# A two-layer block on one core: first stage in parts, first attention unit begun among the last expert tiles, feed-forward steps of the last stage at other places

## The chip, the cores and the metric

The kernel runs on one core of a Trainium2 chip. A core has five engines, each with its own queue of instructions, worked off strictly in order: TensorE (PE in the rows; its weight loads are PEld), VectorE (DVE), ScalarE (ACT), GpSimd (POOL) and SyncE (SP, which here only issues transfers). They wait for each other through semaphores. Data lies in an on-chip buffer of 128 partitions, and TensorE writes into eight accumulator banks. The metric is the time of one execution on the device in microseconds. Three runs of the kernel before took 1812.76, 1813.0 and 1818.22 us, with a median of 1813.0 us.

## The reference

The input is x, 8 sequences of 256 tokens of width 256: 2048 tokens. The program computes two transformer layers, and each adds two branches to its input, both fed by the same layer norm:

```python
xn = layernorm(x)
x = x + L0_attn(xn) + L0_ffn(xn)
xn = layernorm(x)
x = x + L1_attn(xn) + L1_ffn(xn)
```

- `L0_attn` is a delta rule over 16 heads of 128: projections q, k, v, a causal convolution of 4 taps and a SiLU on each, then a recurrence over the tokens, `state += k (beta (v - k state))`, output `q state`, a norm and a projection.
- `L0_ffn` has a shared MLP for every token, and 8 routed experts of which each token uses 2. The router takes a sigmoid of `xn @ router`, chooses two of four groups, then two experts, and weights their outputs.
- `L1_attn` learns at test time: per pair of heads and chunk of 64 tokens it forms gradients of three 128x128 weights, passes each through two Newton-Schulz steps (`A = X X'; B = b A + c A A; X = a X + B X`), adds them to the weights, rescales these, and answers the queries with the new weights.
- `L1_ffn` chooses 2 of 6 experts for each of the 8 sequences: up-projection, GELU, down-projection, weighted sum.

## The kernel before

The order of the work is written out by hand, engine by engine. Each step is a small function of the same name on several engines (TensorE multiplies, ScalarE or VectorE fetches the result from a bank and gives the bank back). The program has these stages, one after the other:

1. **Norm, router, shared MLP** (0 to 109 us). SyncE loads x in four parts of 512 tokens (g = 0 to 3), all counted on one semaphore `s_x`, then 11 small constants, then weights. VectorE waits for all four parts, takes the statistics of all (`norm_stats`, L1866 to L1873), and then normalizes part by part (`norm_rows`, L1882, into `xnr`). GpSimd takes the inverse roots between them (L2583). TensorE turns each part (`ln_turn`, L574, 8 instructions' worth of matmul time per part), and ScalarE and VectorE each fetch one half of it into `xnT` (L1383, L1888). When all parts are turned, TensorE computes the router and beta logits (L621, 64 narrow matmuls). ScalarE takes the sigmoid, and VectorE does the routing, a chain of 38 small dependent instructions (L1924 to L1966), the result of which (`slots`, L1960) lets GpSimd send 2 x 16 blocks of token rows to their slots in device memory (L2594). SyncE then reads the rows back, tile by tile (L500). Meanwhile TensorE works on the shared MLP: `shared_up` (L632, L638), whose result ScalarE passes through SiLU (L1391) and VectorE multiplies (L1977), and `shared_down` (L650). The matmul of the fourth piece (L638) needs the bank that the first of these products gives back, and all the products stand behind the whole routing on VectorE.
2. **Expert tiles** (109 to 207 us). 39 tiles of 128 rows run in a pipeline of four steps on TensorE: `turn_x` (L682), `expert_up` (L690), `turn_h` (L699), `expert_down` (L709). The tile j uses bank j % 2 for its turn.
3. **Layer 0 attention** (207 to some 1360 us). 64 units of 512 tokens and one head, in `period`s in which five units overlap. A unit begins with `project` of queries (QRY), keys (KEY) and values (VAL) on TensorE (L737), the first tap on ScalarE (`tap0`, L1433), three more on VectorE (`tap`, L2020), and the SiLU on ScalarE (L1437). Queries and values share bank 0.
4. **Layer 1 attention and its feed-forward.** 16 units x0 to x15 (a pair of heads and sequences in a chunk), of which four run interleaved. Each unit's Newton steps for s = 0 (two weights at once) and s = 1 (the third) are `TURN` (L1017), `GRAM`, `SQUARE` and `NEXT` (all L1012) on TensorE, with a copy on ScalarE after `TURN` and `GRAM` (L1612, L1615) and an operation on VectorE after `SQUARE` and `NEXT` (L2265, L2268). After them come `turn_weight`, `gate_queries`, `turn_mixed`, `output` and `turn_output`. In the last stretch, from 1719 us, the feed-forward of the eight sequences is laid between the steps of x13 to x15: `up(b)` (L1111) on TensorE, `gelu(b)` on ScalarE (L1661), `weigh(b)` on VectorE (L2188), `down(b)` (L1129, with the output projection of the attention in L1131), and `add_results(b)` (L2194) on VectorE. SyncE begins to load the weights of the chosen experts when unit x12 is out, two experts for each sequence, in four buffers (L541 to L548). A load for sequence b + 4 begins when `down(b)` is done.

ScalarE holds the functions of one table set at a time, and GELU and SiLU lie in different ones: the program has an `ACT_TABLE_LOAD` wherever it goes from one to the other.

## Time and profile before

| | us |
|---|---|
| median of three runs | 1813.0 |
| the profiled execution's own time | 1812.96 |
| its span, first to last instruction | 1811.2 |
| TensorE busy | 1700.7 (94% of the span) |
| VectorE busy | 1493.7 (82%) |
| ScalarE busy | 1199.3 (66%) |
| GpSimd busy | 1102.8 (61%) |

The profile shows one execution. A busy share is an average over stages that have different limits; which wait counts is read from the chain of waits and from the order of time in that stage. The profile also has the clock that was granted to TensorE, as a share of full speed, in any stretch (1.00 is 2.4 GHz, 0.50 is 1.2 GHz).

### The profile page before, as it was taken

The page shows a single profiled execution, that of the slowest core. Times are in us where ns is not written, and L with a number is a line of the kernel's source. Part 1 is how long each engine was busy: PE and PEld are TensorE (multiplying, and loading weights), DVE is VectorE, ACT ScalarE, POOL GpSimd, SP SyncE. Part 2 cuts the span into 40 slices and gives each one's busy share as a digit, 9 for nine tenths or more (in the row PEclk, how much of TensorE's full clock was granted, in tenths as well). Part 3 has the DMA queues.
Part 4 walks back from the last instruction along what each step waited for, and adds up shares of the span by engine and source line. Part 5 has one row for each costly group of instructions (what it writes and reads, how often), then busy time and mean ns, then how long its engine had stood idle before and what let it go on. Part 6 is the DMA issues. An engine that isn't in the chain of part 4 may idle for free.

```text
span 1811.2 us, 41460 instructions
## 1 busy us (share of the span) xinstructions
PE 1700.7 (94%) x14070; PEld 1236.6 (68%) x14070; DVE 1493.7 (82%) x3496; ACT 1199.3 (66%) x2907; POOL 1102.8 (61%) x1148
## 2 busy tenths in 40 slices
PE   5999899999999999999999999999987788888878
PEld 4477557777777777777777777777766566666666
DVE  5322499999999999999999999999986788888843
ACT  1124467777777777777777777777754588778853
POOL 1510057777777777776666666666665578777731
PEclk8999999999999999999999999999988799999999
DMA  9323400110110101100000000011002000000032
GB/s 309 137 83 108 121 22 27 32 38 24 32 35 21 38 20 35 29 24 29 23 18 23 26 15 29 15 26 29 15 1 59 1 1 1 2 1 1 1 89 88
DMA packets 66097, 73.83 MB, mean 41 GB/s; under 512 B 10976, under 2 KB 54768, under 8 KB 65776
## 3 DMA queue, kind: packets, MB, share of 16 engines
q1 hardware_dynamic: 62919, 63.92, 12.2%
q0 software_dynamic: 3072, 8.65, 1.5%
q8 instruction: 49, 0.80, 0.2%
q14 instruction: 57, 0.46, 0.1%
HBM read 55.45 MB, written 17.10 MB: 40 GB/s over the span
## 4 chain that ended last, share of the span: by engine, by line
PE 82%; DVE 8%; ACT 5%; issue 2%; POOL 1%; SPq 1%; DMA 0%; ACTq 0%; POOLq 0%; DVEq 0%
PE banks L737 19%; PE banks L880 6%; PE banks L749 4%; PE banks L836 3%; PE banks L757 3%; PE banks L855 3%; PE banks L765 3%; PE banks L794 3%; PE banks L808 3%; PE banks L690 3%; PE banks L802 2%; PE banks L936 2%; PE banks L801 2%; PE banks L709 2%; PE banks L1012 2%
## 5 line engine op out<-in xcount | busy, mean ns | idle before, releaser
L737 PE MATMUL banks<-xnT,hw 128*128 128x512 f32 x768 | 414.0, 622 | 4.0 <-DVE cv L2020 4.0
L2061 DVE CAST_PREDICATED MM<-lmask,banks 128x512 bf16<-128x512 uint32 x384 | 272.1, 709 | 34.4 <-PE banks L802 30.3
L2020 DVE SCALAR_TENSOR_TENSOR cv<-banks,hc,cv 128x510 f32<-128x510 f32 (+2 forms) x384 | 284.3, 741 | 10.8 <-ACT cv L1433 6.1
L1483 ACT ACTIVATE T<-banks 128x256 bf16<-128x256 f32 x384 | 149.7, 390 | 145.2 <-PE banks L794 144.2
L2665 POOL TENSOR_TENSOR X<-X,yrow 128x512 f32<-128x512 f32 x128 | 163.2, 1275 | 66.5 <-ACT yrow L1515 66.5
L2629 POOL TENSOR_TENSOR kn<-nsum,half_pos 128x4 f32<-128x4 f32 x64 | 65.5, 1023 | 148.5 <-DVE nsum L2032 148.5
L802 PEld LDWEIGHTS banks<-MM,T 128*128 128x128 bf16 x1536 | 104.1, 98 | 65.2 <-issue 48.0
L801 PEld LDWEIGHTS banks<-T,MM 128*128 128x128 bf16 x1280 | 99.0, 97 | 65.4 <-ACT T L1483 63.2
L880 PE MATMUL banks<-ho,OT 128*128 128x256 f32 x512 | 143.1, 403 | 0.0
L794 PEld LDWEIGHTS banks<-MM,Gb 128*128 128x128 bf16 x1536 | 79.2, 98 | 93.7 <-DVE MM L2061 54.0
L2020 DVE SCALAR_TENSOR_TENSOR cv<-banks,hcv,cv 128x510 f32<-128x510 f32 (+2 forms) x192 | 141.2, 736 | 0.8 <-ACT cv L1433 0.7
L1515 ACT ACTIVATE yrow<-banks,oinv 128x256 f32<-128x256 f32 x256 | 107.0, 472 | 50.7 <-POOL oinv L2660 47.8
L802 PE MATMUL banks<-MM,T 128*128 128x64 bf16 x1536 | 136.3, 193 | 0.5 <-ACT T L1483 0.5
L1437 ACT ACTIVATE raw<-cv 128x512 f32<-128x512 f32 x192 | 121.9, 635 | 4.1 <-DVE cv L2020 3.5
L737 PEld LDWEIGHTS banks<-xnT,hw 128*128 128x128 f32 x768 | 116.8, 191 | 8.7 <-issue 6.7
L801 PE MATMUL banks<-T,MM 128*128 128x64 bf16 x1280 | 118.4, 193 | 2.5 <-ACT T L1483 2.5
L794 PE MATMUL banks<-MM,Gb 128*128 128x64 bf16 x1536 | 109.8, 194 | 3.3 <-DVE MM L2061 3.3
L2066 DVE TENSOR_TENSOR Rb<-Rm,banks 128x256 bf16<-128x256 f32 x256 | 106.2, 415 | 5.0 <-POOL Rm L2656 4.1
L2660 POOL TENSOR_TENSOR oinv<-orr,half_neg 128x4 f32<-128x4 f32 x64 | 66.0, 1032 | 52.8 <-ACT orr L1493 52.8
L808 PE MATMUL banks<-Rb,MM 128*128 128x128 bf16 x640 | 89.0, 221 | 6.2 <-DVE Rb L2066 3.8
L880 PEld LDWEIGHTS banks<-ho,OT 128*128 128x128 f32 x512 | 88.3, 192 | 6.9
L1433 ACT ACTIVATE cv<-banks,hc 128x512 f32<-128x512 f32 x128 | 89.2, 697 | 2.4 <-PE banks L737 2.4
(318 smaller groups left out, 4880.7 us busy)
## 6 DMA issues: line engine op xcount, KB each, us to landing
MM<-in_eye SPq DMA_DIRECT2D x64, 256.0 KB, 2.7
slot_rows<-zeros SPq DMA_DIRECT2D x1, 5304.0 KB, 20.4
xs<-slot_rows SPq DMA_DIRECT2D x13, 408.0 KB, 3.9
slot_out<-ye SPq DMA_DIRECT2D x13, 384.0 KB, 2.7
hw<-in_hw SPq DMA_DIRECT2D x16, 256.0 KB, 3.5
wT<-in_winit SPq DMA_DIRECT2D x8, 384.0 KB, 4.5
wgu<-in_wgu SPq DMA_DIRECT2D x1, 2816.0 KB
w1c<-in_ew SPq DMA_DIRECT2D x16, 176.0 KB
```

Of the source, the lines that this page charges most:

```text
L737: ins = pe.matmul(PROJ[t][:], hw[:, kk, t, :], xnT[:, kk, u.b * BLK:(u.b + 1) * BLK], start=(kk == 0), stop=(kk == KD - 1))
L794: last = pe.matmul(o[:, k * 64:(k + 1) * 64], Gb[:, par, k, :], strips(MM[:, u.b, 0, k, :], size, 0, 1), start=True, stop=True)
L801: pe.matmul(o[:, k * 64:(k + 1) * 64], MM[:, u.b, 1, k, :], strips(T1[:, k, :], size, 0, 1), start=True, stop=True)
L802: last = pe.matmul(o[:, (TILES + k) * 64:(TILES + k + 1) * 64], T1[:, k, :], strips(MM[:, u.b, 1, k, :], size, 1, 1), start=True, stop=True)
L808: last = pe.matmul(solve_bank(u)[:, s * P:(s + 1) * P], MM[:, u.b, 1, s * NC + c, :], rhs[:, s, :], start=True, stop=True)
L880: last = pe.matmul(bank[7 - s][:, c * D:(c + 1) * D], OT[:, s * NC + c, :], ho[:], start=True, stop=True)
L1437: act.activation(raw[:, u.b % 2, t, :], cv[:, t, :], ACT.Silu).then_inc(act_silu, 1)
L1483: act.activation(strips(T1[:].rearrange("p i t -> p (i t)"), LEVELS[lv], 0, 1), grams_bank(u)[:, 0:TILES * 64].rearrange("p (k e) -> p k e ...
L1515: last = act.activation(yrow[:, s, c], bank[7 - s][:, c * D:(c + 1) * D], ACT.Copy, scale=oinv[:, u.b % 2, s * NC + c:s * NC + c + 1])
L2020: dve.scalar_tensor_tensor(o, y, taps_of(t)[:, TAPS - 1 - i:TAPS - i], o, ALU.mult, ALU.add).then_inc(dve_conv, 1)
L2061: dve.copy_predicated(dst, m, ps).then_inc(dve_mm, 1)
L2665: pool.tensor_tensor(xs, xs, yrow[:, s], ALU.add).then_inc(pool_x, 1)
```

## The change

**First stage by parts.** Each of the first two parts of x has a semaphore of its own, and the last two share a third. VectorE takes the statistics of part 1 and then normalizes part 0, and so on, instead of all statistics first. ScalarE fetches both halves of every turned part. TensorE computes the logits of part g - 1 behind the turn of part g. VectorE's first two products of the shared MLP stand within the routing instead of behind it.

**First unit.** TensorE projects queries and keys of unit 0 in the tile pipeline's rounds 38 and 39, with the first taps on ScalarE, and the other taps on VectorE around the last `keep_h`. Tiles turn into bank 1 - j % 2, so that the bank of each projection is free. The periods leave these steps out for unit 0.

**Last stage.** The steps `up`, `gelu`, `weigh`, `down` and `add_results` stand at other places between the steps of x13 to x15 on the three engines: `up(0)` and `up(1)` later, and the others around them. Near the end `turn_output(x15)` stands ahead of `up(7)`, and `square_outputs(x15)` and `keep_turned(x15)` ahead of `gelu(6)` and `gelu(7)`.

```diff
@@ loads
-...[:, g * TPB:(g + 1) * TPB, :]).then_inc(s_x, 16)
+...[:, g * TPB:(g + 1) * TPB, :]).then_inc((s_x, s_x1, s_x2, s_x2)[g], 16)
@@ TensorE, first stage
-            for g in range(NBLK):
+            ln_turn(0)
+            for g in range(1, NBLK):
                 ln_turn(g)
+                logits(g - 1)
+            logits(NBLK - 1)
@@ TensorE, tile pipeline
                     expert_up(n - 1, experts[n - 1])
+                if n in (TILES0 - 1, TILES0):
+                    for kk in range(KD):
+                        project(first_unit, QRY if n < TILES0 else KEY, kk)
                 if 0 <= n - 2 < TILES0:
                     turn_h(n - 2)
@@ ScalarE, first stage and tile pipeline
                 act.activation(turned_place(0, 0, g), turned_from(0, 0, g), ACT.Copy).then_inc(ln_kept0, 1)
+                act.activation(turned_place(0, 1, g), turned_from(0, 1, g), ACT.Copy).then_inc(ln_kept1, 1)
...
+                if n in (TILES0 - 1, TILES0):
+                    tap0(first_unit, QRY if n < TILES0 else KEY)
                 if 0 <= n - 3:
                     weigh_y(n - 3)
+                if n == TILES0 + 1:
+                    silu(first_unit, QRY)
+            silu(first_unit, KEY)
@@ VectorE, first stage
+            dve.wait_ge(s_x, 16)
+            norm_stats(0, 0)
+            dve.wait_ge(s_x1, 16)
+            norm_stats(1, 0)
+            norm_rows(0, 0)
+            dve.wait_ge(s_x2, 32)
+            norm_stats(2, 0)
+            norm_rows(1, 0)
+            norm_stats(3, 0)
+            norm_rows(2, 0)
+            norm_rows(3, 0)
...
             step(dve.tensor_scalar(r_w[:], r_w[:], SCALE0, None, ALU.mult))
+            shared_product(0)
...
+            shared_product(1)
             dve.wait_ge(*s_places)
@@ VectorE, tile pipeline
+                if n == TILES0:
+                    tap(first_unit, QRY, 1)
+                    tap(first_unit, QRY, 2)
+            tap(first_unit, QRY, 3)
+            for i in range(1, TAPS):
+                tap(first_unit, KEY, i)
@@ ScalarE, last stage
             newton(x15, 0, 1, TURN)
+            gelu(0)
             newton(x15, 0, 1, GRAM)
             keep_weight(x14, 0)
             keep_turned(x13)
             square_weights(x14, 1)
+            gelu(1)
             keep_weight(x14, 1)
@@ VectorE, last stage
             newton(x14, 1, 1, SQUARE)
+            weigh(0)
             newton(x14, 1, 1, NEXT)
```

How the instructions stand in the built programs, at the places where they move. On TensorE, in the first stage of the kernel before (L574 turns a part, L621 is the logits, L632 and L638 begin the shared MLP):

```order
L574 MATMUL banks<-ident,xnr 128x128 x32
L621 MATMUL banks<-wbr,xnT 128x24 x32
L632 MATMUL banks<-xnT,wsg 128x512 x2
L638 MATMUL banks<-xnT,wsu 128x512 x2
```

and of the changed kernel, where the same steps are L579, L624, L642 and L648:

```order
L579 MATMUL banks<-ident,xnr 128x128 x16
L624 MATMUL banks<-wbr,xnT 128x24 x8
L579 MATMUL banks<-ident,xnr 128x128 x8
L624 MATMUL banks<-wbr,xnT 128x24 x8
L579 MATMUL banks<-ident,xnr 128x128 x8
L624 MATMUL banks<-wbr,xnT 128x24 x16
L642 MATMUL banks<-xnT,wsg 128x512 x2
L648 MATMUL banks<-xnT,wsu 128x512 x2
```

The logits moved up between the turns, and only those of parts 2 and 3 still stand behind the last turn.

On TensorE, at the end of the tile pipeline of the changed kernel (L735 is `project`, L709 `turn_h`, L719 `expert_down`, L700 `expert_up`):

```order
L735 MATMUL banks0<-xnT,hw 128x512 x2
L709 MATMUL banks2<-ident,he 88x128 x2
L719 ISA
L719 MATMUL banks3<-wde,heT 128x256
L719 ISA
L719 MATMUL banks3<-wde,heT 128x256
L700 ISA
L700 MATMUL banks1<-wgu,xT 128x352
L700 ISA
L700 MATMUL banks1<-wgu,xT 128x352
L735 MATMUL banks0<-xnT,hw 128x512 x2
```

In the kernel before, all projections of unit 0 stand behind the last tile (L737 there). Two of the three moved ahead of the last three `turn_h` and `expert_down` steps.

On TensorE, in the last stretch of the kernel before (`XX2`, `banks2` are those of x14, `XX3`, `banks3` those of x15, L936 `gate_queries(x13)`, L1111 `up`):

```order
L936 MATMUL banks1<-w021,qkT1 64x256 x4
L1111 MATMUL banks0<-xnT,w1c 128x256 x4
L1111 MATMUL banks0<-xnT,w1c 96x256 x2
L1017 MATMUL banks2<-identb,XX2 128x128 x4
L1111 MATMUL banks0<-xnT,w1c 128x256 x4
L1111 MATMUL banks0<-xnT,w1c 96x256 x2
L1012 MATMUL banks2<-XX2 128x128 x4
L1017 MATMUL banks3<-identb,XX3 128x128 x8
```

and of the changed kernel, 13 rows further on in the same sequence (L1025 is `GRAM`, `SQUARE` or `NEXT`, L1030 `TURN`, L1093 `turn_output(x13)`, L1072 `turn_weight(x14, 0)`, L1124 `up`):

```order
L1025 MATMUL banks3<-Bm3,XX3 128x128 x8
L1124 MATMUL banks0<-xnT,w1c 128x256 x4
L1124 MATMUL banks0<-xnT,w1c 96x256 x2
L1025 MATMUL banks2<-ln_row 128x128 x4
L1030 MATMUL banks3<-identb,XX3 128x128 x8
L1093 MATMUL banks1<-ident,sg11 128x128 x2
L1025 MATMUL banks2<-Bm2,XX2 128x128 x4
L1025 MATMUL banks3<-XX3 128x128 x8
L1072 MATMUL banks2<-ident,wT2 128x128 x4
L1025 MATMUL banks3<-ln_row 128x128 x8
L1124 MATMUL banks0<-xnT,w1c 128x256 x4
L1124 MATMUL banks0<-xnT,w1c 96x256 x2
```

`up(0)` and `up(1)` moved from right behind `gate_queries(x13)` to behind the first Newton step of x15 and behind its second `SQUARE`.

## Rows read from the trace of the kernel before

**Rows 1.** The page: busy time of TensorE and VectorE.
```profile
PE 1700.7 (94%) x14070; PEld 1236.6 (68%) x14070; DVE 1493.7 (82%) x3496; ACT 1199.3 (66%) x2907; POOL 1102.8 (61%) x1148
```

**Rows 2.** Order of time, first stage: start, duration, engine, instruction, idle before.
```profile
9.64 1.40 DVE L1866 BATCH_NORM_STATS2 ln_st<-X 128x6 f32<-128x256 f32 x4 [9.64 <-DMA X<-in_x]
11.57 1.40 DVE L1866 BATCH_NORM_STATS2 ln_st<-X 128x6 f32<-128x256 f32 x4
21.41 1.37 DVE L1882 TENSOR_SCALAR xnr<-X,ln_mv,ln_rs 128x256 f32<-128x256 f32 x4
26.70 10.12 PE L621 MATMUL banks<-wbr,xnT 128*128 128x24 f32 x64 [0.88 <-DVE xnT L1888]
37.38 0.29 DVE L1924 TENSOR_TENSOR r_sfc<-sig,bias 128x128 f32<-128x128 f32 x1 [10.83 <-ACT sig L1385]
53.55 0.18 DVE L1960 CAST slots<-slotf 128x32 int32<-128x32 f32 x1
55.88 3.78 PE L638 MATMUL banks<-xnT,wsu 128*128 128x512 f32 x4 [3.40 <-DVE hT L1977]
98.36 1.45 SPq L500 DMA_DIRECT2D xs<-slot_rows  x3
108.70 0.60 PE L682 MATMUL banks<-ident,xs 128*128 128x128 f32 x4
```

**Rows 3.** The page's transfers: reading a group of tiles back, us to landing.
```profile
xs<-slot_rows SPq DMA_DIRECT2D x13, 408.0 KB, 3.9
```

**Rows 4.** TensorE in order of time, last stretch.
```profile
1727.87 2.86 PE L1111 MATMUL banks<-xnT,w1c 128*128 128x256 f32 x12 [1.93 <-DMA w2c<-in_eb]
1734.05 4.51 PE L1111 MATMUL banks<-xnT,w1c 128*128 128x256 f32 x12 [3.10 <-DMA w2c<-in_eb]
1745.14 0.62 PE L1012 MATMUL banks<-Bm,XX 128*128 128x128 bf16 x8
1751.03 0.66 PE L1059 MATMUL banks<-ident,wT 128*128 128x128 f32 x4
1800.70 2.84 PE L1129 MATMUL banks<-w2c,hs 128*128 128x256 f32 x12 [0.80 <-DVE hs L2188]
```

**Rows 5.** Transfers of x's four parts, then of wsg: issue to landing, us.
```profile
DMA to landing us min/median/max: 4.3/5.8/7.3
...
DMA to landing us min/median/max: 3.8/3.8/3.8
```

**Rows 6.** Stretches: length, TensorE busy, weight loads busy, granted clock, DMA share, GB/s.
```profile
18.80:20.80 2.00, 1.97 (x10) 1.94 (x11) 1.00 1.12 353
...
27.00:30.00 3.00, 3.00 (x29) 3.00 (x28) 1.00 1.20 429
31.00:34.00 3.00, 3.00 (x16) 3.00 (x15) 0.50 1.05 451
```

**Rows 7.** Weight loads of turns: in the first stage, then among the tiles.
```profile
L574 PEld LDWEIGHTS banks<-ident,xnr x32: 138/226/231, 18.8 to 25.4; 128*128 128x128 f32 x32
...
L682 PEld LDWEIGHTS banks<-ident,xs x66: 139/142/145, 110.6 to 189.9; 128*128 128x128 f32 x66
```

**Rows 8.** The chain of waits: start, duration, what; the first `shared_down`.
```profile
67.49 5.19 PE banks L650 x24
```

**Rows 9.** Order of time around the end of the tiles.
```profile
206.76 3.60 PE L737 MATMUL banks<-xnT,hw 128*128 128x512 f32 x8
210.42 4.53 DVE L2020 SCALAR_TENSOR_TENSOR cv<-banks,hc,cv 128x510 f32<-128x510 f32 x6 [4.93 <-ACT cv L1433]
218.02 3.70 PE L737 MATMUL banks<-xnT,hw 128*128 128x512 f32 x8
```

**Rows 10.** ScalarE and VectorE in order of time, last stretch.
```profile
1729.94 1.28 ACT L1661 ACT_TABLE_LOAD   x1 [3.56 <-PE banks L1111]
1731.24 1.19 ACT L1661 ACTIVATE hg<-banks,w2c 128x256 f32<-128x256 f32 x3
...
1807.91 0.69 DVE L2194 TENSOR_TENSOR X<-X,banks 128x512 f32<-128x512 f32 x1 [2.77 <-PE banks L1131]
```

More of the change, by code:

```diff
@@ L286, in do, with unbegun @@
                 step(u, *which)
+        first_unit = Unit(0, 0, 0)
+        def unbegun(u):
+            return None if u is not None and isinstance(u.n, int) and u.n == 0 else u
         def need(engine, signal, count):
@@ L612, in _, with logits @@
             pe.wait_ge(s_const, 11 * 16)
-            for g in range(NBLK):
-                ln_turn(g)
-            pe.wait_ge(ln_kept0, NBLK + 2)
-            pe.wait_ge(ln_kept1, NBLK + 2)
-            w = NH + E0
-            for t in range(NT):
-                for kk in range(KD):
-                    last = pe.matmul(bank[7][:, t * w:(t + 1) * w], xnT[:, kk, t * P:(t + 1) * P], wbr[:, kk, :],
-                                     start=(kk == 0), stop=(kk == KD - 1))
-            last.then_inc(pe_once, 1)
+            def logits(g):
+                pe.wait_ge(ln_kept0, g + 3)
+                pe.wait_ge(ln_kept1, g + 3)
+                w = NH + E0
+                for t in range(g * TPB, (g + 1) * TPB):
+                    for kk in range(KD):
+                        last = pe.matmul(bank[7][:, t * w:(t + 1) * w], xnT[:, kk, t * P:(t + 1) * P], wbr[:, kk, :],
+                                         start=(kk == 0), stop=(kk == KD - 1))
+                if g == NBLK - 1:
+                    last.then_inc(pe_once, 1)
+            ln_turn(0)
+            for g in range(1, NBLK):
+                ln_turn(g)
+                logits(g - 1)
+            logits(NBLK - 1)
             def shared_up(b):
@@ L710, in expert_down @@
                 last.then_inc(e_dn, 1)
-            experts = {}
-            for n in range(TILES0 + 3):
-                if n < TILES0:
-                    turn_x(n)
-                    experts[n] = pe.value_load(tile_e[0:1, n:n + 1], min_val=0, max_val=E0 - 1)
-                if 0 <= n - 1 < TILES0:
-                    expert_up(n - 1, experts[n - 1])
-                if 0 <= n - 2 < TILES0:
-                    turn_h(n - 2)
-                if 0 <= n - 3:
-                    expert_down(n - 3, experts.pop(n - 3))
             def project(u, t, kk):
@@ L739, in project @@
                     ins.then_inc(pe_proj, 1)
+            experts = {}
+            for n in range(TILES0 + 3):
+                if n < TILES0:
+                    turn_x(n)
+                    experts[n] = pe.value_load(tile_e[0:1, n:n + 1], min_val=0, max_val=E0 - 1)
+                if 0 <= n - 1 < TILES0:
+                    expert_up(n - 1, experts[n - 1])
+                if n in (TILES0 - 1, TILES0):
+                    for kk in range(KD):
+                        project(first_unit, QRY if n < TILES0 else KEY, kk)
+                if 0 <= n - 2 < TILES0:
+                    turn_h(n - 2)
+                if 0 <= n - 3:
+                    expert_down(n - 3, experts.pop(n - 3))
             def tokens(u, t, s, c):
@@ L1306, in _ @@
             turn_weight(x13, 1)
+            newton(x14, 0, 1, NEXT)
             spread_weights()
-            newton(x14, 0, 1, NEXT)
             gate_queries(x13)
-            up(0)
             newton(x14, 1, 0, TURN)
-            up(1)
             newton(x14, 1, 0, GRAM)
@@ L1324, in _ @@
             newton(x15, 0, 0, NEXT)
+            up(0)
             newton(x14, 1, 1, SQUARE)
@@ L1331, in _ @@
             newton(x15, 0, 1, SQUARE)
+            up(1)
             turn_weight(x14, 1)
+            newton(x15, 0, 1, NEXT)
             down(0)
-            newton(x15, 0, 1, NEXT)
             gate_queries(x14)
+            newton(x15, 1, 0, TURN)
             up(2)
-            newton(x15, 1, 0, TURN)
+            newton(x15, 1, 0, GRAM)
             down(1)
-            newton(x15, 1, 0, GRAM)
-            up(3)
             newton(x15, 1, 0, SQUARE)
@@ L1363, in _ @@
             down(5)
+            turn_output(x15)
             up(7)
-            turn_output(x15)
             down(6)
@@ L2003, in keep_h @@
                 dve.tensor_copy(heT[:, j % 2].rearrange("p i t -> p (i t)"), bank[4 + j % 2][0:FH0, 0:2 * P]).then_inc(e_hk, 1)
-            for n in range(TILES0 + 2):
-                if 0 <= n - 1 < TILES0:
-                    expert_h(n - 1)
-                if 0 <= n - 2:
-                    keep_h(n - 2)
             def tap(u, t, i):
@@ L2020, in tap @@
                 dve.scalar_tensor_tensor(o, y, taps_of(t)[:, TAPS - 1 - i:TAPS - i], o, ALU.mult, ALU.add).then_inc(dve_conv, 1)
+            for n in range(TILES0 + 2):
+                if 0 <= n - 1 < TILES0:
+                    expert_h(n - 1)
+                if 0 <= n - 2:
+                    keep_h(n - 2)
+                if n == TILES0:
[4 more added lines that the diff above has]
+                tap(first_unit, KEY, i)
             def key_sums(u, c):
```

115 lines of the change are left out of this document (52 added, 63 removed).

## The prediction, made before the changed kernel ran

> **What bounds the kernel now.** I read the page first: TensorE is busy for 94% of the span [rows 1], so what the change can win lies where TensorE waits or runs at half clock, at the start and at the end. I then read the order of time of the first 110 us, the stretches with their clock, the end of the tiles, and the last stretch engine by engine. In the first stage VectorE starts only when all of x is there, at 9.64. Everything up to the logits' end at 36.82 (26.70 + 10.12) hangs on that, the routing begins at 37.38, and the slots are ready at 53.73 [rows 2]. From there two chains run to the first tile. The sends let the read-back start at 98.36, which lands 3.9 later at 102.3 [rows 2, 3]. TensorE comes at 108.70 [rows 2]. The sends have a slack of 6.4 us. In the last stretch TensorE stands still for 1.93 and 3.10 us before `up(0)` and `up(1)`, until the experts' weights have landed, and all Newton steps are queued behind them [rows 4].
>
> The profiled execution took 1812.96 us, with 1.76 us outside its span, and the median is 1813.0: the sum can be made against either.
>
> **First stage.** The parts of x take 4.3 to 7.3 us from issue to landing [rows 5]. With the first issued at 0.75 us, it lands near 5.1 and the last at 9.64, so about 1.5 us apart. Statistics take 1.93 us a part (11.57 - 9.64) and normalizing takes 1.37 [rows 2]. From 5.1: statistics 0 to 7.0 and 1 to 8.9, rows 0 to 10.3, statistics 2 to 12.2, rows 1 to 13.6, statistics 3 to 15.5, rows 2 to 16.9, rows 3 to 18.3. The first turn also needs the last of the constants. These were issued just before wsg, which went out at 8.23 and landed 3.8 later [rows 5]. I put the constants at 11.0, an estimate.
>
> The first turn of 8 took 2.0 us [rows 6]; eight in a row at that pace (10 in 1.97) take some 1.8 with the last one's end. Logits are 16 matmuls a part: 29 ran in 3.00 us at full clock, so 1.65 us a part, and 16 in 3.00 us at half clock, so 3.0 a part [rows 6]. Over all 64 it was 10.12 us, or 2.5 a part [rows 2]. All slow: turn 0 to 13, turn 1 to 15.5, then logits, turn, logits, turn, logits, logits without a gap, 4 x 3.0 + 2 x 1.8 = 15.6, ends at 31.1. All fast, the last turn can begin at 18.3 and is followed by 1.2 + 2 x 1.65: 22.8. Which one? The granted clock reads 1.00 from 18.8 to 20.8, but a turn's weight load takes 226 ns there and 142 ns among the tiles, and the thin logits themselves were followed by 0.50 [rows 6, 7]. The durations decide for me: TensorE is slow in the first turns. But the logits took 2.5 a part, partly fast. By that figure for them the end is 15.5 + 4 x 2.5 + 2 x 1.8 = 29.1, and with the last two turns as short as the clock allows (1.4 less, by 142 ns against 226) 27.7. I take 28.3, 8.5 us earlier than 36.82.
>
> A rule bears on that row. The Trainium skill, TensorE: Matmul & The Clock Gate, part 1, says that the throttled state is the default and that activity releases it, and it warns that the trace's clock events are not always to be trusted. By that rule the turns start slow, as I took them. By the granted clock alone the logits would end at 22.8 and the sum would be 5.5 us less.
>
> Next, what the two products add. The chain from the first routing instruction to the slots took 53.73 - 37.38 = 16.35 us [rows 2]. The products are about as wide as the taps (0.76 us each [rows 9]), and a small part of them fills VectorE's wait for the counts of TensorE: 1.0 us more, bounds 0.8 and 1.5. That makes 17.35. The slots then come at 28.3 + 0.56 + 17.35 = 46.2, 7.5 us earlier. TensorE gains more: the wait of 3.40 before the fourth piece and the half clock behind it go. From the beginning of that wait, 55.88 - 3.40 = 52.48, to the first `shared_down` at 67.49 there are 20 matmuls in 15.0 us [rows 2, 8], and at 0.45 us each (3.60 for eight [rows 9]) they take 9.0. So TensorE arrives 8.5 + 6.0 = 14.5 us earlier, at 94.2. The sends arrive 7.5 earlier, at 94.8. They are now the later ones, and the first tile starts 108.7 - 94.8 = 13.9 us earlier. Bounds: 13.9 - 2.8 if the logits end at 31.1, 13.9 + 5.5 if at 22.8. No more than that is lost below unless the sends themselves get slower, since the moved instructions add no transfer. SyncE's queue holds the same transfers in the same order.
>
> **First unit.** Queries and keys are 8 of the matmuls of 0.45 us that stood behind the tiles (3.60 us) [rows 9]. They now stand between them. TensorE is full there, so the tiles end 3.6 us later, at 210.3 by the clock of the kernel before. What is gained is that the first tap, the three taps and the SiLU of the queries run beside the last tiles. VectorE does the taps at 0.76 us each (4.53 for six) [rows 9]. Two of them are in front of the last `keep_h`, which holds `expert_down(38)` by about 0.5 us. The query taps end at 210.4, the key taps at 212.8, the key SiLU at 213.4, the values' first tap at 214.1 (it stands behind that SiLU on ScalarE), and their three taps at 216.4. Unit 1's projection waits for that and began at 218.02 [rows 9]. That gives 1.6 us. Bounds: 2.7 if only the key chain counted, and -0.5 if the held `expert_down` and the late store of the last tiles cost as much as the chain wins. I take 1.6, from the row that the next unit waits on.
>
> **Last stage.** Removed from the path behind `gate_queries(x13)`: 1.93 + 2.86 + 3.10 + 4.51 = 12.4 us [rows 4]. Not all of that time is free. VectorE's scaling of x15 and the squares of x14's weights on ScalarE were finished in its shadow, and are late next: about 1.4 us. So `NEXT(x15, 0, 0)`, which ended at 1745.76, ends 11 us earlier, at 1734.8. Then `up(0)` and `up(1)` come back at full clock, 2.7 us each (the second ran at 4.51, slowed). `gelu(0)` stands on ScalarE ahead of x15's second `GRAM` copy, and needs 1.28 us for its table and 1.19 for itself [rows 10]: 2.2 us of new wait on TensorE. Other waits of some 1.9 us are covered by `up(0)`. At `turn_weight(x14, 1)`, which ended at 1751.69 [rows 4], I get -11.0 + 5.4 - 1.9 + 2.2 = -5.3 us. Behind it the remaining waits, the 0.80 before `down(6)` [rows 4] and some 2 us of small ones, are covered by feed-forward steps, and new ones cost about 0.5: -7.7. The weights of every sequence land before its `up`, since each `down(b)` that frees a buffer comes earlier too. I count some thirty hand-offs between engines at nothing in this walk, so I take -6.8. The last addition on VectorE, at 1807.91 [rows 10], then starts at 1801.1. Bounds: -11 if all small waits go, +1 if each of `gelu(0)` to `gelu(2)` holds the Newton steps behind it for its full 2.5 us and the later covers fail (-6.8 + 3 x 2.5 = +0.7).
>
> A rule speaks against this part. The Trainium skill, ScalarE: Activation LUTs, What ACT_TABLE_LOAD costs, gives a drain of 1.38 us besides the load of 1.28. In this trace the GELU starts 0.02 us behind the load [rows 10], so I count no drain. By the rule two exposed loads would make the sum 2.8 us more, 1793.5.
>
> **Sum.** 13.9 + 1.6 + 6.8 = 22.3, and 1813.0 - 22.3 = 1790.7 us.
>
> **Rivals.**
> 1. *TensorE is fast in the first stage.* The granted clock of 1.00 speaks for it [rows 6], the weight loads of 226 ns against it [rows 7]. The logits end at 22.8: 1790.7 - 5.5 = 1785.2 us.
> 2. *The last stage gives its gain back.* `weigh(b)` stands on VectorE ahead of Newton steps and waits for a GELU that waits for a table. TensorE's two waits of 5.0 us and the slow 1.7 us become waits of the Newton steps behind ScalarE. The load of 1.28 and the GELU of 1.19 [rows 10] speak for it, that these steps are queued once for each GELU. Against it, TensorE has an `up` or `down` of 2.7 to 3.5 us to do at most of them. Only 1 us is left of 6.8, and 1796.5 us comes out.
> 3. *The sends get slower.* They now begin at 47 us, while SyncE's bulk loads still run (DMA shares of 1.1 early on [rows 6]). If a quarter of the 32 sends take 0.5 us longer, the first tile starts 4 us later: 1794.7.
> 4. *Slower than before.* The 60 or so steady periods between 220 and 1360 us are bound by TensorE and by VectorE closely behind (94% and 82% [rows 1]). Unit 0 now enters with its queries and keys done, and the code before the loop has another length. If the units settle into another phase, or the loop's instructions are fetched later, each period pays. From 22.3 / 60 = 0.37 us per period on the kernel is slower; at 0.5 us it takes 1790.7 + 30 = 1820.7 us. Against it: the loop's text is the same, all its waits are between units, and a late start leaves no mark after one unit.
> 5. *The parts don't help*: if the constants, not x, held the first turn until 18 us, the first stage would win only the overlap of the logits and the products: some 6 us less, 1797. The landing of wsg at 12.0 [rows 5], behind them, speaks against it.
>
> **How the numbers follow.** The forecast, 1790.7, has 0.50; rival 1 0.13, rival 2 0.17, rival 3 0.10, rival 4 0.04, rival 5 0.04; no effect, by losses that cancel, 0.02. The forecast's own range, from the constants and the hand-offs, is 1787 to 1795. For 8 in 10 I take 1783 to 1800, which leaves out the lowest end of rival 1, the worst of rivals 2 and 3 together, and rival 4. A measurement of this kernel tells 0.3%, 5.4 us, from no change: faster 0.94, within it 0.02, slower 0.04.
>
> **What would show it.** In the changed profile: statistics from 5.1 us; the first turn at 11; the last logits at 28 with turn loads of 226 ns; the slots at 46; no wait before the fourth L648 matmul; the first tile (L692) at 95 with TensorE idle for 0.6 us before it; unit 1's projection 15.5 us earlier than 218.0; `up(0)` without a wait; ScalarE's `GRAM` copy behind the GELU's table load; the last addition on VectorE at 1785.6. It is wrong if the turns start after 13 us, if the tiles start before 92 or after 98, if the periods' length differs by more than 0.05 us, or if the last stretch shortens by less than 3 us.

## The result, and the profile after

| | median of its runs | ratio to before, 95% interval | profiled execution |
|---|---|---|---|
| before | 1813.85 us (6 runs, 1812.72 to 1818.22) | | 1812.96, span 1811.2 |
| changed | 1792.86 us (6 runs, 1791.16 to 1802.52) | 0.9891 [0.9876, 0.9906] | 1802.52, span 1800.7 |

The forecast was 1790.7 us (1783 to 1800). The change brings 21.0 us between the medians, or 1.09%.

The profiled execution is the slowest of the six, 9.7 us over their median. Lines of its page:

```profile
span 1800.7 us, 41462 instructions
PE 1710.1 (95%) x14070; PEld 1245.5 (69%) x14070; DVE 1490.8 (83%) x3492; ACT 1202.2 (67%) x2911; POOL 1104.9 (61%) x1148
PEclk9999999999999999999999999999987699999999
```

TensorE's busy time rose by 9.4 us against [rows 1], although it does the same 14070 matmuls. Where the same work takes longer, look at the clock. TensorE in order of time, first stage (start, duration, engine, line, what, idle before and who ended it):

```profile
11.48 3.72 PE L579 MATMUL banks<-ident,xnr 128*128 128x128 f32 x16 [11.48 <-DMA moec<-in_moec]
15.00 3.45 PE L624 MATMUL banks<-wbr,xnT 128*128 128x24 f32 x16
25.02 6.86 PE L624 MATMUL banks<-wbr,xnT 128*128 128x24 f32 x32
...
97.75 0.41 PE L692 MATMUL banks<-ident,xs 128*128 128x128 f32 x2 [0.93 <-DMA xs<-slot_rows]
98.63 0.43 PE L692 MATMUL banks<-ident,xs 128*128 128x128 f32 x2 [0.47 <-issue]
99.42 2.62 PE L700 MATMUL banks<-wgu,xT 128*128 x4 [0.35 <-issue]
```

The order is as forecast: first turn at 11.5, logits between the turns, rows from the sends as the last wait. But 16 logits took 3.45 us, 0.215 a piece, and the logits ended at 31.88, not at 28.3. Before they took 0.158 a piece [rows 2]. The first tile begins at 97.75 instead of 108.70, 10.95 us earlier. Behind the wait of 0.93 the first tiles are slow (2.62 us for the four that took 1.45 before); the granted clock is 0.61 from 99.4 to 103.8, and 1.00 behind it.

The second place is after the loop, two stretches in each of the two kernels (length, TensorE busy, clock, share of the transfers, GB/s); first before, then changed:

```profile
1420.00:1430.00 10.00, 7.57 (x44) 0.50 0.00 0
1430.00:1440.00 10.00, 6.43 (x71) 0.99 0.00 0
```
```profile
1420.00:1430.00 10.00, 7.22 (x53) 0.67 0.00 0
1430.00:1440.00 10.00, 9.22 (x64) 0.62 0.01 2
```

The changed kernel was 9.98 us ahead of the kernel before at its 1424 and 4.98 us ahead at its 1438, at the same instructions. Four matmuls of 512 columns that took 1.94 us before take 3.60 here (L960). Nothing in the change touches this place.

The last stretch, TensorE, then ScalarE:

```profile
1717.13 0.36 PE L1021 MATMUL banks<-gsum,onesP 128*128 128x12 f32 x2 [0.41 <-DVE gsum L2266]
...
1729.93 2.81 PE L1124 MATMUL banks<-xnT,w1c 128*128 128x256 f32 x12
...
1737.94 1.03 PE L1025 MATMUL banks<-ln_row 128*128 128x128 bf16 x8 [2.35 <-ACT ln_row L1635]
1738.77 4.08 PE L1124 MATMUL banks<-xnT,w1c 128*128 128x256 f32 x12
...
1796.40 1.03 PE L1144 MATMUL banks<-wpj,oT 128*128 128x256 f32 x4
```
```profile
1733.45 1.02 ACT L1632 ACTIVATE XX<-banks 128x1024 bf16<-128x1024 bf16 x1 [3.35 <-PE banks L1030]
1734.49 1.28 ACT L1681 ACT_TABLE_LOAD   x1
1735.78 1.19 ACT L1681 ACTIVATE hg<-banks,w2c 128x256 f32<-128x256 f32 x3
1736.87 1.02 ACT L1635 ACTIVATE ln_row<-banks 128x1024 bf16<-128x1024 f32 x1
```

The waits of 1.93 and 3.10 us of [rows 4] are gone. The forecast new wait behind `gelu(0)` is there, 2.35 us, and `up(1)` behind it takes 4.08 us instead of 2.81, at a granted clock of 0.64. From `total(x15)` (1717.13) to the end of `down(7)` it is 80.30 us. Before, these were at 1722.10 and 1807.87, 85.77 us.

One place marks the loop in both kernels: GpSimd's norm of the keys, once a unit (count, shortest/median/longest ns, start of the first and last); before, then changed:

```profile
L2629 POOL TENSOR_TENSOR kn<-nsum,half_pos x64: 1006/1027/1049, 219.2 to 1331.6; 128x4 f32<-128x4 f32 x64
```
```profile
L2656 POOL TENSOR_TENSOR kn<-nsum,half_pos x64: 1007/1029/1051, 208.6 to 1322.5; 128x4 f32<-128x4 f32 x64
```

### The profile page after: what moved, and what is told of

It is laid out like the page before. It is cut to its first block, busy times and chain, and to the rows that moved or that the text cites. A ratio compares the mean times of both kernels' runs of the same rounds, so it can differ in the third digit from the quotient of the medians.

```text
span 1800.7 us, 41462 instructions
## 1 busy us (share of the span) xinstructions
PE 1710.1 (95%) x14070; PEld 1245.5 (69%) x14070; DVE 1490.8 (83%) x3492; ACT 1202.2 (67%) x2911; POOL 1104.9 (61%) x1148
## 4 chain that ended last, share of the span: by engine, by line
PE 80%; DVE 9%; ACT 5%; POOL 3%; issue 2%; DMA 1%; SPq 0%; POOLq 0%; DVEq 0%; ACTq 0%
PE banks L735 19%; PE banks L893 6%; PE banks L762 4%; PE banks L770 3%; PE banks L849 3%; PE banks L868 3%; PE banks L778 3%; PE banks L807 3%; PE banks L821 3%; PE banks L700 3%; PE banks L815 2%; PE banks L949 2%; PE banks L814 2%; PE banks L1025 2%; PE banks L719 2%
## 5 line engine op out<-in xcount | busy, mean ns | idle before, releaser
L735 PE MATMUL banks<-xnT,hw 128*128 128x512 f32 x768 | 414.1, 622 | 2.5 <-DVE cv L2034 2.5
L735 PEld LDWEIGHTS banks<-xnT,hw 128*128 128x128 f32 x768 | 116.9, 191 | 6.5 <-DVE cv L2034 3.1
```

The source lines that it names most:

```text
L735: ins = pe.matmul(PROJ[t][:], hw[:, kk, t, :], xnT[:, kk, u.b * BLK:(u.b + 1) * BLK], start=(kk == 0), stop=(kk == KD - 1))
```

## The experiments

Twelve kernels ran, in four sets on four chips (B to E; the first two profiles are of A). Each set timed the kernel before as well: medians 1824.1 (B), 1822.2 (C), 1814.3 (D), 1823.7 (E). Because chips differ by 10 us, ratios are compared, and the profiles are cut at marks: end of the routing logits, start of the last send, first tile's turn, first and last norm of the keys, `total(x15)`, end of `down(7)`. The first three columns are times from the start, the other four are lengths from one mark to the next, in us.

| kernel | chip | ratio [95%] | logits end | last send | first tile | to 1st norm | loop | to total | last stretch |
|---|---|---|---|---|---|---|---|---|---|
| before | A | | 36.8 | 95.8 | 108.7 | 110.5 | 1112.4 | 390.5 | 85.8 |
| before_again | C | (one run, 1817.39) | 38.3 | 97.2 | 112.9 | 110.5 | 1112.5 | 390.7 | 85.8 |
| changed | A | 0.9891 | 31.9 | 91.8 | 97.8 | 110.9 | 1113.9 | 394.6 | 80.3 |
| after_again | C | 0.9882 [0.9858, 0.9906] | 24.0 | 83.9 | 100.9 | 108.6 | 1113.9 | 394.5 | 80.3 |
| e1_first_stage | B | 0.9933 [0.991, 0.9956] | 23.9 | 83.8 | 98.1 | 111.8 | 1114.0 | 389.2 | 85.7 |
| e2_first_unit | B | 0.9985 [0.9968, 1.0002] | 36.7 | 95.7 | 118.7 | 108.7 | 1113.7 | 391.9 | 89.3 |
| e3_last_stage | B | 0.9964 [0.9946, 0.9981] | 39.1 | 98.6 | 119.3 | 110.5 | 1112.4 | 394.5 | 80.3 |
| e4_warm | B | 0.9888 [0.9863, 0.9912] | 27.6 | 87.5 | 103.4 | 108.6 | 1113.9 | 394.6 | 80.3 |
| e5_gelu_later | C | 0.9891 [0.9868, 0.9914] | 31.7 | 91.6 | 104.7 | 108.7 | 1112.7 | 394.0 | 79.1 |
| e6_warm_short | C | 0.9892 [0.9869, 0.9915] | 23.5 | 83.4 | 97.6 | 108.6 | 1112.7 | 389.0 | 78.7 |
| e7_gelu_earlier | D | 0.9863 [0.9841, 0.9884] | 24.0 | 83.9 | 89.7 | 111.9 | 1113.6 | 392.0 | 77.9 |
| e8_half_sends | D | (one run, 1794.51) | 31.7 | 69.6 | 97.5 | 108.7 | 1113.7 | 390.8 | 78.7 |
| e9_both | D | 0.9878 [0.9859, 0.9898] | 23.9 | 83.9 | 89.8 | 110.9 | 1113.7 | 390.8 | 77.9 |
| e10_no_idle | E | 0.9877 [0.9855, 0.9899] | 23.5 | 83.4 | 103.2 | 108.7 | 1113.4 | 390.5 | 77.9 |

**The three parts alone.** Each is the kernel before with that part's hunks of the diff and no others.

> The kernel before with the first stage's edits alone (x by parts, the routing logits of a block behind the turns of the next, both copies of the turned rows on ScalarE, two products of the shared expert within the routing). Theory A (the prediction's term, 13.9 us): 1813.9 - 13.9 = 1800.0. Theory B (what the profile of the changed kernel shows at its first expert tile, 97.75 against 108.70, 10.95 us, with nothing given back behind it): 1802.9. Theory C (the tiles begin in a half-clock stretch in every execution, since TensorE waits 0.93 us for the rows right before them; 2.3 us given back): 1805.2. Rival D: the period of the loop hides the earlier start, no change, 1813.9. In the profile: logits end at 31.9, slots at 49.6, first tile turn at 97.7 if A's clock assumption was the wrong step.

> The kernel before with the first unit's edits alone (the projections of queries and keys of unit 0, their taps and silu, between the last expert tiles; the two banks of the turned rows swapped). Theory A (the prediction's term): 1.6 us earlier, 1812.3. Theory B (profile of the changed kernel: from the first tile to unit 1's projection 109.7 us against 109.3, of which 2.3 are a half-clock stretch, so 1.9 gained): 1812.0. Rival C: the swap of the banks or the projections between the tiles cost what they bring, 1813.9. In the profile: unit 1's first projection at about 216.2 instead of 218.02.

> The kernel before with the last stage's new order alone. Theory A (the prediction's term): 6.8 us, 1807.1. Theory B (profile of the changed kernel: 5.6 us gained behind the last loop, 1.3 more lost in up(1) at half clock behind the wait of 2.35 for ScalarE's copy, which came behind gelu(0)): 1808.3 where the half-clock stretch comes every time, 1807.0 where it doesn't. Rival C: the last stage gives most of it back, 2 us or less, 1812 or more. In the profile: wait of about 2.3 us before SQUARE(x15,0,1), and none over 0.7 us on TensorE behind it.

The gains are 0.67%, 0.15% and 0.36%, or 12.2, 2.7 and 6.5 us of 1813.9, each to about 0.2% (4 us); the forecast's terms were 13.9, 1.6 and 6.8. Their sum is 1.18% (21.4 us), and the whole gives 1.09 and 1.18%: within that noise the parts add up. The first unit's interval includes no gain, so its claim rests on its stretch in the profile: 110.5 becomes 108.7, 1.8 us. The last stage's stretch goes from 85.8 to 80.3. In e2 the last stretch is 89.3 with unchanged code there. That is the clock: 0.92 in it against 0.98 before, with 4.1 us more of busy time (an `up` of 5.49 and one of 3.91 us) and no more idle time.

e1 was a surprise. The same code as in the changed kernel ended its logits at 23.9:

```profile
11.28 3.81 PE L574 MATMUL banks<-ident,xnr 128*128 128x128 f32 x16 [11.28 <-DMA moec<-in_moec]
14.89 1.97 PE L619 MATMUL banks<-wbr,xnT 128*128 128x24 f32 x16
20.23 3.65 PE L619 MATMUL banks<-wbr,xnT 128*128 128x24 f32 x32
```

Sixteen logits in 1.9 us, not 3.45. Still the first tile came at 98.1, since TensorE stood still again and again with nothing to wait for ("issue"), and ScalarE got signals late ("remote"; up to 15.8 us behind the end of the matmuls that its SiLU waits for). The same is in the changed kernel's second profile.

**The changed kernel again, and the kernel before again.**

> The changed kernel as it is, for a second profiled execution. Its first one took 1802.5 us, 9.7 over the median of its runs (1792.9). Theory A: the excess is half-clock stretches of TensorE that fall by chance: routing logits end at 31.9 instead of the 23.9 that the kernel with the first stage's edits alone showed, 2.3 us in the first two tiles, 5.0 us between 1425 and 1440, 1.3 in up(1). Then in this profile the logits end at 24 to 28 or the stretch near 1430 is short, and profile and median agree within 3 us. Theory B: the stretches belong to the kernel (a wait right before each brings them): logits end at 31.9 and the stretch near 1430 is again 9 us longer than in the kernel before. Ratio to the kernel before 0.989 by both.

> The kernel before as it is, for a second profiled execution beside the others of this chip. On the last chip it took 1824.1 us against 1813.9 on the first, and three kernels showed there a stretch in which TensorE's matmuls came 0.3 to 1.5 us apart with nothing to wait for (about 8 us in all, from some 8 us before the last row send to 3 us behind it). Theory A: the slower chip shows that stretch in the kernel before too, at 88 to 100 us: a time near 1824 with it, near 1814 without it. Rival B: it comes only where the sends start earlier: none here, whatever the time.

Theory A holds for the logits: 24.0. The stretch near 1430 was long again (394.5), as theory B says, though e1, e6, e8, e9 and e10 were without it (389.0 to 390.8) and e2 and e7 had a part of it (392). The five long ones are all kernels with the new last stage, and five of ten profiles with that order have it, none of four without. That is too few to tell a cause from chance, and the trigger stays open. TensorE of after_again during the sends, then ScalarE:

```profile
67.65 1.88 PE L642 MATMUL banks<-xnT,wsg 128*128 128x512 f32 x4
...
79.74 1.02 PE L642 MATMUL banks<-xnT,wsg 128*96 128x512 f32 x2 [1.29 <-issue]
82.56 1.31 PE L648 MATMUL banks<-xnT,wsu 128*96 128x512 f32 x2 [1.37 <-issue]
84.69 0.59 PE L648 MATMUL banks<-xnT,wsu 128*96 128x512 f32 x1 [0.81 <-issue]
```
```profile
68.45 0.59 ACT L1406 ACTIVATE sg<-banks 96x512 f32<-96x512 f32 x1 [2.25 <-remote]
88.32 1.56 ACT L1406 ACTIVATE sg<-banks 128x512 f32<-128x512 f32 x3 [19.27 <-remote]
```

The SiLU at 88.32 needs the four matmuls that began at 67.65 and ended at 69.5: its signal came 18.8 us late. Such gaps are in all nine profiles of chips B, C and E, the kernel before among them (rival B of its expectation is out), and in none of the five of A and D. They end 3.4 to 4.6 us behind the start of the last send in each of the nine. On those chips TensorE, held up by them, and not the sends, sets the first tile: it follows TensorE's last product without a wait, 13 to 23 us behind the last send. On A and D it can follow 5.9 us behind. The kernel before took 1817.4 us with the gaps, not 1824 as theory A had it: they explain 4.1 us at its first tile (112.85 against 108.70), and not all of the 8 to 10 us between the chips' medians.

**Making TensorE warm.** Before the first turn:

```
+            pe.wait_ge(*s_half)
+            for n in range(26):                # e6, e9: 16
+                pe.matmul(bank[5][:, 0:ROW], zeros[:, 0:P], zeros[:], start=True, stop=True)
             pe.wait_ge(s_const, 11 * 16)       # e6, e9: 2 * 16, identity and routing weights;
                                                # the wait for the others stands before the last logits
```

> The changed kernel with 26 matmuls of zeros (128 by 272 columns, result unused) on TensorE from about 1.3 us on, in the time in which it waits for the constants (first turn at 11.48). Theory A: in the changed kernel the first stage's turns (0.22 us each) and logits (0.215 us each) ran at 1.2 GHz because TensorE came to them idle; busy before them it is at 2.4 GHz, a turn takes 0.12 and a logits matmul 0.156 us as in the full-clock rows of the kernel before; then the turns wait for the normalised rows (last ones at 18.2), logits end near 24 to 26 instead of 31.9, and the run takes 1786 to 1788 against 1792.9. Rival B: it is the narrow matmuls themselves (24 columns out) that bring the clock down whatever goes before: logits still end at 31 to 32, 1792 to 1794. Rival C: matmuls of zeros at half clock take 0.46 us each, all 12 us, and the clock stays low: first turn at 13.5 instead of 11.5, 1795.

> The changed kernel with 16 matmuls of zeros (not 26) on TensorE from about 1.4 us on, and its first turn waiting for the identity and the routing weights alone, not for all eleven constants. Theory A: in the run with 26 the matmuls of zeros took 15.1 us (0.58 us a piece until 8, 0.4 after), so the first turn came at 16.4 instead of 11.5, and turns and logits ran at full clock nevertheless (0.12 and 0.11 us a piece), logits ending at 27.5. With 16 they end at 9.5 to 10.5, the first turn starts at 10 to 10.5, logits end at 23 to 24.5, bounded by the normalised rows (18.2) in every execution. Against the changed kernel: 0 us where its logits ran at full clock anyway, 3 to 8 where not: ratio 0.985 to 0.989. Rival B: the half clock returns in the shared expert's first matmuls (as in the kernel before, 36.6 to 41) and the sends, not TensorE, set the first tile: no change, 0.989. Profile: logits' end, slots' end, first tile.

In e4 the matmuls of zeros took 15.10 us (52 records): some 0.41 us each until 8 us and 0.21 behind 10 us, with a granted clock that reads 1.00 in both. By the durations that is half and full clock. They held the first turn until 16.36, and turns and logits then ran at full clock. Rival B is out: narrow matmuls alone do not bring the clock down in this order (in the kernel before, it was 0.50 from 31 to 34 us, within its 64 logits in a row [rows 6]). In e6 they ended just before the first turn, at 11.31, so the early constants had nothing to give, and the logits ended at 23.5. Three of three kernels with these matmuls had fast logits, and four of seven without (e1, after_again, e7, e10; slow in the changed kernel, e5, e8). That is too few to call it a cure, and the ratios (0.9888, 0.9892) show no gain.

**gelu(0) one step later, one step earlier.** On ScalarE, from the changed kernel:

```
             newton(x14, 1, 1, GRAM)
+            gelu(0)                            # e7, e9, e10: earlier
             newton(x15, 0, 1, TURN)
-            gelu(0)
             newton(x15, 0, 1, GRAM)
+            gelu(0)                            # e5: later; weigh(0) behind SQUARE(x15, 0, 1)
```

> The changed kernel with gelu(0) one step later on ScalarE (behind its copy of ln_row for x15,0,1) and weigh(0) behind the steps that this copy releases on VectorE. Theory A: TensorE's wait of 2.35 us before SQUARE(x15,0,1) at 1737.94 goes, nothing late takes its place since down(0) comes 5 us later, and up(1) runs at full clock (2.81 against 4.08): 2.3 to 3.6 us faster than the changed kernel, ratio to the kernel before 0.9872 to 0.9879 where the changed kernel's is 0.9890. Rival B: gelu(0) then stands before keep_weight(x14,0), weigh(0) and down(0) come late by the 2.5 us of its table load and activations, no gain: 0.989. Profile: start of down(7) 63.9 us (A) or 66.3 us (B) after SQUARE(x15,0,0)'s neighbour up(0)'s start as in the changed kernel (1729.93 to 1793.80).

> The changed kernel with gelu(0) one step earlier on ScalarE, in front of its copy of the turned x15,0,1, in the 3.35 us in which ScalarE waits there (1730.10 to 1733.45). Theory A: its table load (1.28 us) runs in that wait, its activations end at 1733.1 behind up(0), so the wait of 2.35 us before SQUARE(x15,0,1) goes and up(1) finds TensorE busy and runs at full clock (2.81 instead of 4.08 us): from TensorE's total(x15) to the end of down(7) 76.6 to 77.5 us against 80.3 in three runs of the changed kernel (and 79.1 where gelu(0) came later, with the wait moved to up(1)). Ratio to the kernel before 0.986 to 0.987. Rival B: the wait moves again, to up(1) or to turn_weight(x14,1), 79 to 80.3 us, ratio 0.989. Rival C: the copy of x15,0,1 comes late by gelu(0)'s length, 82 us.

In e5 the wait moved one step on, to `up(1)`, which needs the bank that `gelu(0)` reads:

```profile
1739.27 0.62 PE L1025 MATMUL banks<-ln_row 128*128 128x128 bf16 x8 [0.67 <-ACT ln_row L1635]
1741.86 2.83 PE L1124 MATMUL banks<-xnT,w1c 128*128 128x256 f32 x12 [1.98 <-ACT hg L1681]
```

It gained 1.2 us, no more than the clock of `up(1)` (2.83 for 4.08): rival B in the main. At the same clock this order is the slower one: e6 and e8, with `gelu(0)` where the changed kernel has it and full clock in the whole stretch, have 78.7 against 79.1. In e7 the load came into ScalarE's idle time, though later in it than expected. The table load waits with its activation for `up(0)`'s first result (1.85 us), so the copy was late and 1.27 us of wait are left:

```profile
1722.05 1.28 ACT L1681 ACT_TABLE_LOAD   x1 [1.85 <-PE banks L1124]
1723.34 1.19 ACT L1681 ACTIVATE hg<-banks,w2c 128x256 f32<-128x256 f32 x3
1724.43 1.02 ACT L1632 ACTIVATE XX<-banks 128x1024 bf16<-128x1024 bf16 x1
```
```profile
1725.50 0.62 PE L1025 MATMUL banks<-XX 128*128 128x128 bf16 x8 [1.27 <-ACT XX L1632]
1727.69 2.81 PE L1124 MATMUL banks<-xnT,w1c 128*128 128x256 f32 x12
```

The last stretch is 77.86 us, 2.44 less and not quite the 76.6 to 77.5 of theory A, and exactly that again in e9 and e10. Only 0.80 us of the 2.44 is shown to come from the order. e6 has `gelu(0)` where the changed kernel has it, the same wait, and full clock behind it:

```profile
1728.70 0.62 PE L1028 MATMUL banks<-ln_row 128*128 128x128 bf16 x8 [2.36 <-ACT ln_row L1638]
1729.16 2.81 PE L1127 MATMUL banks<-xnT,w1c 128*128 128x256 f32 x12
```

Its last stretch is 78.66, and e8's too, with 7.8 us of idle time on TensorE against 7.0 in e7, e9 and e10. The other 1.64 us is the clock. Whether the new place keeps it up is not shown: the four profiles with 80.3 are all of the kind with the long stretch near 1430, and e6 to e10 are not; the fifth of that kind, e5, has full clock with `gelu(0)` later. The ratio of 0.9863 is the lowest of all, but its interval overlaps the changed kernel's, and e9 and e10 with the same edit have 0.9878 and 0.9877. So 0.8 us in the profile carries the claim.

**Half of the sends.** On GpSimd, and on SyncE in front of the tiles' loads:

```
-            for t in range(NT):
-                send(t, 1)
...
             sp.wait_ge(e_first, 16 * NT)
-            sp.wait_ge(e_second, 16 * NT)
+            sp.wait_ge(e_sent, 1)
```

> The changed kernel without the second 16 of the 32 row sends of GpSimd (every token's row goes to the first of its experts alone; the tiles are loaded after the first 16). On two chips the profiles show TensorE's matmuls of the shared expert 0.2 to 1.7 us apart with nothing to wait for, and VectorE and ScalarE getting TensorE's signals 3 to 19 us late, until 3.4 to 4.4 us behind the last send in eight of eight profiles; on a first chip neither. Theory A (the sends do it): with the last send at 62 to 70 TensorE runs without a gap from 67 to 75 us on, and the shared expert ends at 90 or before. Rival B (something else that falls in this time, the writing of zeros or the loading of weights, or the length of TensorE's work in a row): gaps again between 70 and 92. On a chip as the first, no gaps at all and nothing learned.

Without the second sends the tiles lack rows and the results are other ones, so only the order of time counts here. It fell on a chip without gaps, so it says nothing on them, and whether the sends cause them stays open. It shows one other thing: with the tiles' rows read back from 72.43 on, the first tile began at 97.47, when TensorE was done. With slow logits TensorE comes as late as the rows (97.75).

**Everything together, and no idle time.** e9 is the changed kernel with the edits of e6 and e7. e10 is e7 with, on TensorE:

```
             shared_down(NBLK - 1)
+            for n in range(2):
+                pe.matmul(bank[5][:], ident[:], xnT[:, n, 0:BLK], start=True, stop=True)
```

> The changed kernel with the 16 matmuls of zeros, the early first turn and gelu(0) one step earlier. Theory A: the first tile at 97.6 as in the run with the matmuls of zeros alone (97.8 and 100.9 in the changed kernel), the last stretch 76.6 to 77.5 us instead of 80.3: ratio to the kernel before 0.985 to 0.987, the fastest of all. Rival B: the stretches at half clock that fall by chance (5 us near 1430, 1.5 in the loop) hide it: 0.989.

> The kernel with gelu(0) one step earlier (ratio 0.9863 in its run), and two matmuls whose result nobody reads (128 by 512 columns, 0.86 us each at full clock) between the shared expert's last product and the first expert tile. Where the row sends end at 84.8, TensorE otherwise waits there for the tiles' rows (1.86 us in that kernel's profile, 0.70 and 0.93 in two others), and in all three the next 4 to 6 us run at 1.2 GHz: 6.98 us from the first tile's turn to the first turn of the products, against 3.64 without such a wait (six profiles). Theory A: it is the idle time right before that brings the clock down; with it filled, 3.6 to 3.7 us, first tile at 89.8 to 90.0, and from the first tile to the first unit's norms 108.6 instead of 111.9: 3.0 us faster, ratio 0.9846. Rival B: the clock falls at this place anyway, since the tiles' narrow matmuls follow: 6 to 7 us, ratio 0.9863 or up to 1.7 us more. Rival C: in executions where TensorE is late (logits at half clock, or gaps during the sends) the first tile comes 1.7 us later and nothing is saved: ratio 0.987.

e9 has the shortest span, 1786.3, but not the best ratio: 0.9878, short of its theory A (0.985 to 0.987). e10 got a chip with gaps. TensorE came late anyway, the two matmuls cost their 1.7 us (rival C), and the question it was made for was not put. What the profiles say of it: where TensorE waited for the rows, the next tiles were slow. e7's:

```profile
89.73 0.41 PE L692 MATMUL banks<-ident,xs 128*128 128x128 f32 x2 [1.86 <-DMA xs<-slot_rows]
91.43 2.71 PE L700 MATMUL banks<-wgu,xT 128*128 x4
94.36 2.56 PE L700 MATMUL banks<-wgu,xT 128*128 x4
```

From the first tile's turn to the first turn of the products it is 6.98 us in e7, and 6.04 and 6.07 in the changed kernel and e9, all behind a wait for the rows. It is 3.64 in the eleven others. The granted clock over these stretches is 0.53, 0.72 and 0.72, and 1.00 in each of the eleven. That the wait is the cause was not tested, and a wait alone does not do it: behind the 2.36 us before `up(1)` in e6 the clock stayed at 1.00.

## Why the prediction came out right, point by point

**The sum.** The profiled execution of the changed kernel is its slowest, so I look for one that stands for the median. e7's profiled execution is its median (1790.15). Take it, put the changed kernel's last stretch in for its own (+2.44), and set it against the kernel before. First tile 108.70 to 89.73: -19.0. To the first norm +1.4. The loop +1.2. To `total` +1.5. Last stretch -5.5. Together -20.4, a span of 1790.8 and with the 1.8 us outside 1792.6. The measured median is 1792.86. That fits a usual run with fast logits, but it does not show one. e8 had slow logits, a first tile at 97.5, full clock in the tiles and in the last stretch, and took 1794.51 us; with e6's way to `total` (389.0 for 390.8) that would be 1792.7, and with the slow tiles on top (2.4) 1795.1. So a run with slow logits can lie as near to the median, and what the usual run has stays open.

- *First stage, 13.9 us: right in size for a wrong reason.* The failed step is "I take 28.3" for the end of the logits. I mixed a slow and a fast piece time, as the kernel before did (29 logits in 3.00 us, then 16 in 3.00 [rows 6]). In the new order there is no mixture in any of ten profiles: all 64 logits run at one pace, and where no matmuls of zeros hold them up they end at 31.7 to 31.9 or at 23.5 to 24.0. 28.3 lay between, so its nearness to the mean was luck. At the first tile the gain is 10.95 or 19.0 us on a chip without gaps. Of the 19.0, 3.3 go back in the slow tiles (6.98 against 3.64), which leaves 15.7; of the 10.95, 2.4 go back (6.04), which leaves 8.6. The upper bound, 19.4, holds; the lower, 11.1, was too high. In the changed kernel's own profile the later signs slipped with it: slots at 49.60 for 46, unit 1's projection at 207.46, 10.6 us earlier than before and not 15.5, and the last addition at 1797.47 for 1785.6.
- *Turn loads at 226 ns while the clock reads 1.00* decided for slow turns. That was right for the first turns (16 in 3.72 us). In the changed kernel's profile the granted clock reads 1.00 from 20 to 34 us, with the logits at 0.215 us, and in after_again's too, with 0.11. The Trainium skill, TensorE: Matmul & The Clock Gate, part 1, warns that the trace's clock events are not to be fully trusted. The trace agrees: in the first stage of these two profiles the durations tell the pace and the granted clock does not.
- *The products, +1.0, chain 17.35.* From the first routing instruction (32.44) to the slots (49.60) it is 17.16. Right. The wait of 3.40 before the fourth piece is gone, as forecast.
- *The sends bind, TensorE idle 0.6 us.* Right: 0.93 us. That the tiles behind this wait took 2.4 us more (6.04 against 3.64) was not in the sum.
- *First unit, 1.6 us.* 1.8 us (110.48 to 108.65). Right.
- *Last stage, 6.8 us.* 5.5 us. The term for `gelu(0)`, 2.2 of new wait, measured 2.35. Missing was the clock behind it: 1.27 us in `up(1)` and 0.4 in the Newton step (e6 and e8, with the same order and the same wait, have 78.7, a gain of 7.1 us). I had written "at full clock, 2.7 us each".
- *Rival 1* (logits at 22.8) came at the logits in four of seven profiles without matmuls of zeros (23.5 to 24.0). By the sum above it comes to 1792.6 and not to 1785.2 even so, because the slow tiles (3.3), the loop and the way to `total` (2.7) and the last stage (1.3) give it back. *Rival 2* is out. *Rival 3*: the sends kept their pace, 41.3 us from the first to the last (50.53 to 91.83; before 54.66 to 95.84, 41.2). *Rival 4*: the loop takes 1.0 to 1.7 us more in nine of the eleven profiles of kernels with one of the early parts or both, 0.3 in e5 and e6. That is some 0.02 us a unit, where 0.37 would have been needed. *Rival 5* is out: the first turn was at 11.5.
- *The ACT_TABLE_LOAD drain* of 1.38 us that the Trainium skill gives (ScalarE: Activation LUTs, What ACT_TABLE_LOAD costs) does not appear. In the changed kernel ScalarE's copy ends at 1734.47, the load runs from 1734.49 to 1735.77, and the GELU starts at 1735.78: 0.02 us before the load and 0.01 behind it. The measurement decides.

## What to carry to other kernels

Where TensorE comes from idle, sum up a stage once at either clock and give both times. The ten profiles of the new first stage were one or the other, and the kernel before went from one to the other within its turns and its logits [rows 6, 7]; a mean is right only by luck. A short wait in front of dense work can cost more than its length: here the tiles behind a wait of 0.70 to 1.86 us took 2.4 to 3.3 us more, and `up(1)` behind a wait of 2.35 took 1.3 more in some executions and nothing more in others. So give a new wait that you accept two prices. A step moved off one wait lands on the next: look for the idle time of the engine that must do it (3.35 us on ScalarE here), and remember that a table load waits with its activation. And before you credit an edit with a shorter stretch, compare it with a run without the edit at the same clock: of e7's 2.44 us only 0.80 was the order.

## What the runs showed of the hardware that was not expected

- The same code runs its first logits at 0.11 or at 0.215 us a piece in different executions, with a granted clock of 1.00 in both records.
- On three of five chips TensorE's matmuls come 0.2 to 1.7 us apart, and its signals reach ScalarE up to 19 us late, in the time of GpSimd's indirect sends. The medians of the kernel before are 1822 to 1824 us on these chips and 1814 on the two without gaps; in the one pair of profiles of that kernel the gaps cost 4.1 us at the first tile.
- The same steps near 1430 us, from one unit's `gsum` matmuls to the next, take 19.7 to 19.8 us in seven profiles (granted clock 1.00), 21.4 in two (0.92) and 24.9 to 25.0 in five (0.73), with the same code there.
